# Router with high and low weights side by side, spare rows stored by slot, and loads moved at both ends of an attention and mixture-of-experts kernel

## What is computed

```python
xn = _layernorm(x)
# attention: 16 heads of 32, causal
P = softmax(where(causal, Q @ K.T * scale, -1e30)); out = (P @ V) @ Wo.T
# router: 8 experts in 4 groups of 2, the best 2 groups, then the best 2 experts
logits = xn @ rw.T
scores = sigmoid(logits)
sfc = scores + bias
...
topk_w = topk_w / (sum(topk_w) + 1e-20) * 2.5
# each expert, and a shared one of double width (704)
y_e = (silu(xn @ gate_e.T) * (xn @ up_e.T)) @ down_e.T        # 352 wide
```

## Time and profile before

| | |
|---|---|
| median of 3 runs | 1050.87 us |
| the three runs | 1046.09, 1050.87, 1958.02 us |
| the profiled execution | 1046.42 us |
| its span | 1044.7 us |
| busy: PE, DVE, ACT, POOL | 981.6, 725.4, 678.2, 533.8 us |
| granted PE clock, mean | 0.982 |

### The profile page before, as it was taken

One profiled execution on the slowest core, in us unless ns is written; L12 is line 12 of the kernel. 1 busy time (PEld: TensorE's weight loads), 2 busy tenths in 40 slices (PEclk: granted clock), 3 DMA queues, 4 the chain that ended last, 5 costly groups with the idle time before them and its releaser, 6 DMA issues. The chain is left out here.

```text
span 1044.7 us, 18885 instructions
## 1 busy us (share of the span) xinstructions
PE 981.6 (94%) x5176; PEld 808.7 (77%) x5177; DVE 725.4 (69%) x1436; ACT 678.2 (65%) x1419; POOL 533.8 (51%) x573
## 2 busy tenths in 40 slices
PE   5999988999999999999999999988879999999994
PEld 4767877787787877777777877766679999999993
DVE  6741332667687788888898888753467777777771
ACT  3332211278788897888888878871167777777771
POOL 0010840768788877876666766751013444434421
PEclk9999989999999999999999999999899999999997
DMA  6989897644787867969868778538889545465432
GB/s 202 331 320 383 228 205 266 204 134 96 192 159 172 174 138 177 202 143 268 247 199 247 206 247 199 171 117 290 294 283 310 100 91 123 93 173 89 77 59 38
DMA packets 136491, 199.69 MB, mean 191 GB/s; under 512 B 63088, under 2 KB 81776, under 8 KB 132816
## 3 DMA queue, kind: packets, MB, share of 16 engines
q1 hardware_dynamic: 126064, 177.88, 59.8%
q0 software_dynamic: 9760, 20.49, 10.6%
q10 hardware_dynamic: 576, 0.26, 0.2%
HBM read 117.11 MB, written 73.08 MB: 182 GB/s over the span
## 5 line engine op out<-in xcount | busy, mean ns | idle before, releaser
L1448 POOL TENSOR_TENSOR prob_lo<-prob,prob_hi 128x512 fp32r<-128x512 f32 (+2 forms) x320 | 329.7, 1048 | 127.1 <-ACT prob_hi L1492 114.8
L1485 ACT ACTIVATE prob<-ps_s 128x512 f32<-128x512 f32 (+3 forms) x384 | 188.1, 490 | 70.9 <-PE ps_s L1729 50.0
L1492 ACT ACTIVATE prob_hi<-prob 128x512 fp32r<-128x512 f32 (+3 forms) x384 | 199.4, 520 | 12.4 <-ACT row_stage L1466 12.4
L1581 DVE CUSTOM_DVE_ANT_0 ps_m<-ps_m,causal 128x384 f32<-128x384 f32 (+3 forms) x256 | 125.4, 497 | 55.3 <-PE ps_m L1700 48.5
L2140 DVE TENSOR_TENSOR rw_lo<-gu_sb,rw_hi 128x704 fp32r<-128x704 f32 x156 | 135.8, 892 | 34.7 <-ACT rw_hi L2072 32.6
L2072 ACT ACTIVATE rw_hi<-gu_sb 128x704 fp32r x156 | 123.5, 794 | 32.0 <-issue 21.8
L2045 POOL DMA_INDIRECT out<-work,slot_table x39 | 64.5, 1654 | 155.3 <-ACT work L2102 94.1
L1724 PE MATMUL ps_s<-qs,ks 97*128 97x512 f32 (+3 forms) x384 | 136.3, 355 | 3.2 <-DMA qs<-max_rows 2.2
L1700 PE MATMUL ps_m<-ks,qs 96*128 96x512 f32 (+3 forms) x384 | 131.3, 342 | 5.6 <-DVE maxima L1581 5.5
L1747 PE MATMUL ps_o<-prob_hi,vs 128*66 128x512 f32 (+3 forms) x384 | 130.0, 339 | 1.3 <-POOL prob_lo L1448 1.3
L1749 PE MATMUL ps_o<-prob_lo,vs 128*66 128x512 f32 (+3 forms) x384 | 129.3, 337 | 0.0
(11 more groups left out here) (207 smaller groups left out, 2358.3 us busy)
## 6 DMA issues: line engine op xcount, KB each, us to landing
xt<-xt_blocks SPq DMA_DIRECT2D x7, 2048.0 KB, 8.5
v_rows<-work SPq DMA_DIRECT2D x16, 512.0 KB, 3.1
xt_blocks<-xt SPq DMA_DIRECT2D x4, 2048.0 KB, 11.3
qk_hi<-work SPq DMA_DIRECT2D x8, 1024.0 KB, 4.5
qk_lo<-work SPq DMA_DIRECT2D x8, 1024.0 KB, 7.3
qs<-qk_hi SPq DMA_DIRECT2D x64, 128.0 KB
ks<-qk_hi SPq DMA_DIRECT2D x64, 128.0 KB
vs<-v_rows SPq DMA_DIRECT2D x32, 256.0 KB
```

Source lines behind the costliest of these rows:

```text
L1448: nc.gpsimd.tensor_tensor(prob_lo[:, s % NPL, 0:w], prob[:, s % NP, 0:w], prob_hi[:, s % NPH, 0:w].bitcast(F32), ALU.subtract).then_inc(lo ...
L1485: nc.scalar.activation(prob[:, s % NP, 0:w], bank("score", s)[:, 0:w], ACT.Exp, scale=SCALE).then_inc(exp_done, 1)
L1492: nc.scalar.activation(prob_hi[:, s % NPH, 0:w], prob[:, s % NP, 0:w], ACT.Copy).then_inc(hi_ready, 1)
L1581: nc.vector.tensor_tensor_reduce(ps_m[s % NM][:, 0:w], ps_m[s % NM][:, 0:w], causal[:, TBW - w:], 1.0, MASKED, ALU.add, ALU.max, maxima[:, ...
```

## The change

1. In norm_phase wv is loaded before tile 2 of x instead of before tile 1.
2. `r_hi` and `r_lo` become the two halves of `r_parts`, 16 columns. Each block takes 8 matmuls of 16 stationary columns. The copies, the transposes and the PSUM tile `ps_s` are 16 wide. VectorE copies one half of the turned logits and adds the other to it, at the head of its evacuation of chunk 1, and ScalarE's sigmoid waits for that.
3. The spare rows are made in a tile of their own, [39, 128, 2], one partition for each tile of slots, and stored as 39 rows of 1 KB at the same step.
4. The tiles of `out` for the first two steps of out_phase are loaded into `y_first` at the end of attend_phase, behind wo. out_phase doesn't load them again.
5. The first experts' loads are cut: gate, up, first down part, second down part at steps 4, 5, 6, 7 for expert 0 and 8, 9, 10, 11 for expert 1.

```diff
-FIRST_AT = [5, 9]
+FIRST_AT = [(4, 5, 6, 7), (8, 9, 10, 11)]
...
-        r_hi = ctx.enter_context(nc.sbuf_tensor("r_hi", [P, KC, E], F32R))
-        r_lo = ctx.enter_context(nc.sbuf_tensor("r_lo", [P, KC, E], F32R))
+        r_parts = ctx.enter_context(nc.sbuf_tensor("r_parts", [P, KC, 2 * E], F32R))
...
+            y_first = nc.alloc_sbuf_tensor_at("y_first", [P, 2, D], F32,
+                                              offset=nc.sbuf_base + 4 * TBW * KC)
...
+def load_matrix(eng, e, n, matrix, gu_sb, expert_loaded):
+    eng.dma_start(gu_sb[:, e * KC:(e + 1) * KC, n * F:(n + 1) * F],
+                  matrix[e * KC:(e + 1) * KC].rearrange("k p f -> p k f")
+                  ).then_inc(expert_loaded[e % len(FIRST_AT)], 16)
...
+def load_down_part(eng, e, part, down_dram, d_ring, down_loaded):
+    n, w, at = e % DOWN_SLOTS, FCH[-1][1], part * len(FCH)
+    eng.dma_start(d_ring[:, n, at:at + 2, :].bitcast(F32), down_dram[e, :, part, 0:2, :]
+                  ).then_inc(down_loaded[n], 16)
+    eng.dma_start(d_ring[0:w, n, at + 2, :].bitcast(F32), down_dram[e, 0:w, part, 2, :]
+                  ).then_inc(down_loaded[n], 16)
...
-                    if t == 1:
+                    if t == 2:
+
                         for k in range(KC):
                             sp.dma_start(wv_raw[:, k, :], wv[:, k, :]).then_inc(wv_loaded[k], 16)
...
-                        sp.dma_start(slots_dram.rearrange("(j p) a -> p j a", p=P),
-                                     slot_table[:, :, :]).then_inc(pads_stored, 16)
+                        sp.dma_start(slots_dram.rearrange("(j p) a -> j p a", p=P),
+                                     pads[:, :, :]).then_inc(pads_stored, 16)
...
                         if t == 1 and n == 1:
-                            act.wait_ge(logits_turned, 1)
-                            nc.scalar.activation(score[:, :, :], ps_s[:, :, :],
+                            act.wait_ge(logits_summed, 2)
+                            nc.scalar.activation(score[:, :, :], score[:, :, :],
                                                  ACT.Sigmoid).then_inc(score_ready, 1)
...
-                        for a, part in ((r_hi, 0), (r_lo, 0), (r_hi, 1)):
-                            last = nc.tensor.matmul(ps_r[0:E, :], a[:, k, :], xt[n][:, part, k, :],
-                                                    start=(j == 0), stop=(j == 3 * KC - 1))
+                        for part in range(2):
+                            last = nc.tensor.matmul(ps_r[0:2 * E, :], r_parts[:, k, :],
+                                                    xt[n][:, part, k, :],
+                                                    start=(j == 0), stop=(j == 2 * KC - 1))
...
-                nc.gpsimd.iota(pads[:, :], pattern=[[0, 1]], base=T, channel_multiplier=1
+                nc.gpsimd.iota(spare_rows[:, :], pattern=[[1, P]], base=T, channel_multiplier=0
                                ).then_inc(table_padded, 1)
-                nc.gpsimd.memset(slot_table[:, :, 1], 0.0).then_inc(table_padded, 1)
+                nc.gpsimd.memset(pads[:, :, 1], 0.0).then_inc(table_padded, 1)
                 pool.wait_ge(table_padded, 2)
-                nc.gpsimd.tensor_copy(slot_table[:, :, 0].bitcast(I32),
-                                      pads[:, :].broadcast_to([P, NST])).then_inc(table_padded, 1)
+                nc.gpsimd.tensor_copy(pads[:, :, 0].bitcast(I32), spare_rows[:, :]
+                                      ).then_inc(table_padded, 1)
...
                         dve.wait_ge(logits_turned, 1)
+                        nc.vector.tensor_copy(score[:, :, :], ps_s[:, :, E:]
+                                              ).then_inc(logits_summed, 1)
+                        dve.wait_ge(logits_summed, 1)
+                        nc.vector.tensor_tensor(score[:, :, :], ps_s[:, :, 0:E], score[:, :, :],
+                                                ALU.add).then_inc(logits_summed, 1)
...
+                def load_first_tokens():
+
+                    sp.wait_ge(acc_stored, 64 * (UNITS - NTB + 1))
+                    for t in range(OUT_AHEAD):
+                        sp.dma_start(y_first[:, t, :], out[t * P:(t + 1) * P, :]
+                                     ).then_inc(x_loaded[t], 16)
...
+                    if t < R:
+                        return
                     wait(sp, added, t - U + 1)
                     sp.dma_start(y_tile[:, c, :], out[bass.ds(t * P, P), :]).then_inc(x_loaded[c], 16)
...
-                    if isinstance(t, int) and t in FIRST_AT:
-                        e = FIRST_AT.index(t)
-                        load_expert(sp, e, gate, up, gu_sb, expert_loaded)
-                        load_down(sp, e, down_dram, d_ring, down_loaded)
+                    for e, at in enumerate(FIRST_AT):
+                        for n, matrix in enumerate((gate, up)):
+                            if t == at[n]:
+                                load_matrix(sp, e, n, matrix, gu_sb, expert_loaded)
+                        for part in range(2):
+                            if t == at[2 + part]:
+                                load_down_part(sp, e, part, down_dram, d_ring, down_loaded)
...
+                    tokens = y_first if t < R else y_tile
+                    nc.vector.tensor_tensor(y_sum[:, c, :], ps_y[c % R][:, :], tokens[:, c, :],
                                             ALU.add).then_inc(added, 1)
```

More of the change, by code:

```diff
@@ L187, in moe_attention_kernel @@
                 norm_phase(nc, x, wv, wqk, xt, w_raw, w_loaded, ident, v_dram, xn_dram, out, work,
-                           v_stored, xn_stored, zeros_stored, router, r_hi, r_lo, passed, x_loaded)
+                           v_stored, xn_stored, zeros_stored, router, r_parts, passed, x_loaded)
                 second_half = Half(*[finish_ctx.enter_context(
@@ L219, in moe_attention_kernel @@
                 nc.sbuf_tensor("y_tile", [P, YS, D], F32) as y_tile:
-            out_phase(nc, finish, wo_hi, wo_lo, out_hi, out_lo, a_hi_ready, a_lo_ready, gate, up, down_dram, ident, work, gu_sb, d_ring, out, y_tile, y_stored,
+            out_phase(nc, finish, wo_hi, wo_lo, out_hi, out_lo, a_hi_ready, a_lo_ready, gate, up, down_dram, ident, work, gu_sb, d_ring, out, y_tile, y_first, y_stored,
                       slot_table, xn_dram, gathered, passed, expert_loaded, w_loaded, x_loaded)
@@ L323, in row_numbers @@
     return bass.IndirectOffsetOnAxis(slot_table[:, j, 0:1].bitcast(I32), 0)
+def load_matrix(eng, e, n, matrix, gu_sb, expert_loaded):
+    eng.dma_start(gu_sb[:, e * KC:(e + 1) * KC, n * F:(n + 1) * F],
+                  matrix[e * KC:(e + 1) * KC].rearrange("k p f -> p k f")
+                  ).then_inc(expert_loaded[e % len(FIRST_AT)], 16)
 def load_expert(eng, e, gate, up, gu_sb, expert_loaded):
[L327 to L330, removed]
+    for n, matrix in enumerate((gate, up)):
+        load_matrix(eng, e, n, matrix, gu_sb, expert_loaded)
 def downs_loaded(e):
@@ L338, in downs_loaded @@
     return W_BEFORE + raw + 64 * (e // DOWN_SLOTS + 1)
+def load_down_part(eng, e, part, down_dram, d_ring, down_loaded):
[4 more added lines that the diff above has]
+                  ).then_inc(down_loaded[n], 16)
 def load_down(eng, e, down_dram, d_ring, down_loaded):
-    n, w = e % DOWN_SLOTS, FCH[-1][1]
     for part in range(2):
[L345 to L349, removed]
+        load_down_part(eng, e, part, down_dram, d_ring, down_loaded)
 def norm_phase(nc, x, wv, wqk, xt, w_raw, w_loaded, ident, v_dram, xn_dram, out, work, v_stored,
-               xn_stored, zeros_stored, router, r_hi, r_lo, passed, x_loaded):
+               xn_stored, zeros_stored, router, r_parts, passed, x_loaded):
     with ExitStack() as ctx:
@@ L590, in project_phase @@
         bias_b = sbuf("bias_b", [P, 1, E])
-        pads = sbuf("pads", [P, 1], I32)
+        spare_rows = sbuf("spare_rows", [NST, P], I32)
+        pads = sbuf("pads", [NST, P, 2])
         score = sbuf("score", [P, NT, E])
@@ L604, in project_phase @@
         ps_r = psum("ps_r", [P, TBW])
-        ps_s = psum("ps_s", [P, NT, E])
+        ps_s = psum("ps_s", [P, NT, 2 * E])
         ps_rank = psum("ps_rank", [P, NT, E])
```

25 lines of the change are left out of this document (14 added, 11 removed).

## The result

The changed kernel took 1036.28 us in the median of six runs (1034.43 to 1040.53). The kernel before took 1051.48 beside them, also in the median of six: five from 1045.71 to 1053.69 and one of 1958.02. The ratio is 0.985, its 95% interval 0.982 to 0.988. The forecast was 1030.5 with a range of 1022 to 1040, and "within 2%" at 0.79. The time lies in the range and in the likeliest class, 5.8 us above the forecast and 1.3 above the forecast's own range. In this series the measured gain, 15.2 us, is close to the sum of the forecast, 15.9, and what was off is the time from which the sum was subtracted.

A forecast was written before the change was run, and what follows sets the result against it. It took TensorE (PE) as the bound, at 94% of its span, and subtracted 1.2 + 3.7 + 6.0 + 5.0 = 15.9 us from 1046.4 to get 1030.5. Its own range was 1027 to 1035, widened by rivals to 1022 to 1040.

The forecast's parts named there:

- A: Kernel start: loading wv after the second x tile brings the first value matmul from 14.11 to 12.9; gain 1.2 us.
- B: Projection: the 16-column router needs 16 fewer matmuls at 0.232 us each; gain 3.7 us, from 2.3 to 3.7.
- C: Projection: storing spare rows by slot removes a stall of 3.42 us standing and 2.6 at lower clock; gain 6.0 us.
- D and E: Output stage: two out tiles loaded early (D, 0 to 0.3 us) and first experts' loads cut (E); gain 5 us.
- no y_tile wait over 2 us: Output stage: sign expected for the early tiles and cut loads, no wait for a y_tile load above 2 us.
- 9 us are to be had: Output stage: PE's loss to expert loads, 5.24 + 1.40 us standing and 2.3 at the lower clock level.
- some 4.5 us of the 9 stay: Output stage: loss expected to remain because DMA at 334 GB/s needs 3.7 us per step where PE wants 2.80.
- (2): Output stage: short waits lower PE's clock over three or four tiles, taking the stage's gain; about 1036 us, chance 0.10.
- (3): Output stage: clock stays at the lower level from tile 5 to 15, slower than before; 1051.7 us, chance 0.02.
- Rival (1): Output stage: DMA engines carry some 400 GB/s, no wait is left, 9 us gained; 1026.5 us, chance 0.14.
- The base: Whole kernel: the time subtracted from, the profiled execution's 1046.4 us, instead of the median shown, 1050.87.
- Attention and the routed stage keep their lengths within 2 us: Attention and routed experts: sign that these stages change by at most 2 us; the prediction is wrong if they move.

The follow-up runs named there:

- e4: The changed kernel with twelve 8-column router matmuls per block again and no sum of halves; 1040.65 us.
- e2: The kernel before with only the spare rows stored by slot; 1049.14 us, ratio 0.9925.
- e5: The kernel before, unedited, run once more for a second profile; 1055.45 us (one run).
- e9: The kernel before, unedited, timed against itself in twelve runs; 1055.13 us, ratio 0.998.
- e3: The kernel before with only the first experts' loads cut into steps 4 to 11, without the early load of out tiles; 1049.3 us, ratio 0.997.
- e1: The changed kernel, unedited, run again for a second profile; 1036.68 us, ratio 0.980 to the kernel before.
- e8: The changed kernel, unedited, run a third time; 1036.11 us, ratio 0.981 to the kernel before.
- e7: The changed kernel with attention's 2 MB loads of turned tokens cut into four of 512 KB, three steps apart; 1036.1 us.
- e6: The changed kernel with expert 1's four load pieces at steps 12 to 15 instead of 8 to 11; 1035.15 us, ratio 0.979 to the kernel before.
- e10: The changed kernel with the experts' load pieces at steps 2, 4, 6, 8 and 10, 12, 14, 15; 1034.2 us, ratio 0.978 to the kernel before.

## Why the prediction was right

**What bounds the kernel.** Right within what the profiles tell: the time of PE standing or slow that the edits removed came off its stages, 6.15 us for a forecast 6.0 in projection and 4.3 in the output stage, where PE's losses fell by 4.5.

**A.** "Gain 1.2." The first pair gave 0.9 at the first value matmul (14.11 to 13.20). Over all profiles the five with the old start had it at 13.66 to 14.17 (mean 13.98), the nine with the new one at 11.61 to 13.20 (mean 12.15): 1.8 us, and as much at the first router matmul. Right in kind and inside its ends, 0.6 too small. The term is tile 2's landing: I put it at 10.2, and VectorE took the tile up at 9.05 to 10.64, 9.60 in the mean.

**B.** "3.7." Right: 3.7 in e4's profile, and 4.0 in the medians, which spread more than that. The pitch stayed, and VectorE's two operations (0.29 each) delayed neither PE nor ScalarE: none of their listed waits in the stage is for them.

**C.** "Gain 6.0; ends 3 and 6.3." Right: 6.15 in the projection of e2; 6.9 us (1056.01 to 1049.14) in the medians. The upper end was read from one draw of the stall: PE stood 3.42 us for it in the first profile and 4.53, 4.42 and 5.43 in the other three with the old store (e5, e9, e3). The stores of chunks 3 and 4, which I saw as next late, held nobody. The landing of the new store, put at 3 to 5 us, isn't recorded; that no wait on `ps_q` is left and 288 GB/s move from 124 to 140 is what shows it harmless. One sign failed, "a granted clock of 1.00 there": it was 0.83 in the stage's first 10 us, though not by the store. It costs about 1.5 us, and that is why the pair of profiles shows 8.3 us where B and C measured 3.7 + 6.15.

**D and E.** "Gain 5; ends 1 and 9." Measured 4.3 in the first pair, 4.6 and 4.5 with e1 and e8 against the same profile; e4 and e7, with the same output stage, would give 2.3 and 4.0. What D gives (forecast 0 to 0.3) is lost in that spread. The sign "no y_tile wait over 2 us" failed by one wait of VectorE, 2.59 us, with PE never held as long. Seven more waits at VectorE's add, 14.8 us in sum, are listed without what ended them; that the pieces hold the steps is shown by e6 and e10, which only moved them. The terms can be read from PE's pitches. One held step of the kernel after, PE in the timeline:

```profile
725.02 0.40 PE L1975 MATMUL ps_ay<-wo_lo,a_hi 128*128 128x512 f32 x1
725.25 0.40 PE L1975 MATMUL ps_ay<-wo_hi,a_lo 128*128 128x512 f32 x1
726.04 0.50 PE L1975 MATMUL ps_ay<-wo_hi,a_hi 128*128 128x512 f32 x1 [0.39 <-DVE a_lo L1936]
726.38 0.39 PE L1975 MATMUL ps_ay<-wo_lo,a_hi 128*128 128x512 f32 x1
```

Pitches are 0.233 us when nothing holds PE. Here they are 0.79 and then 0.34: 0.56 + 0.11 = 0.67 us lost, where the bracket reads 0.39. Each restart costs some 0.27 us beyond its idle time: 0.40 - 0.233 = 0.17, since a matmul lasts longer than the pitch, and 0.11 for the slower first pitch. Summed in this way over the steps that were held, seven of them (two too short to be listed), the kernel after loses 4.9 us. In before the two stalls lose 7.1 by the same reading and the slow stretch behind the first 2.3 more (11 pitches in 4.86 us, 733.28 to 738.14, where 2.56 would do): 9.4. So "9 us are to be had" was 9.4, "some 4.5 us of the 9 stay" was 4.9, and 9.4 - 4.9 = 4.5 against 4.3 measured. The second figure is right by two errors that cancel. The engines carried more than the 334 GB/s that I took: 385, 345, 379, 374 and 353 in the five windows that had loads to the end, 367 in the mean, so PE idled less, 2.8 us listed. And I counted nothing for restarts, seven times 0.27 or 1.9 us.

That short waits leave the clock alone held in this stage: after five waits of up to 0.8 us, seven in e3 and seven of up to 1.07 in e4, it read 1.00. Rivals (2) and (3) fell with that. The frequent short idle times between groups that the Trainium skill (TensorE: Matmul & The Clock Gate, A second HAM failure mode: psum-queue depth-cycling) describes as making the clock swing did not do so here. It isn't a matter of length alone: 1.13 us in attention was followed by 0.50 in e9 and by 1.00 in the profile before. Rival (1) was half right on the rate and wrong on "no wait is left"; e10 reached that by giving the pieces room.

**The base: the step that was off.** "The lowest, 1046.09, agrees with the profiled one, so I forecast from there." Two executions that agree and happen to be the fast ones are no base for a median. 1051.48 - 15.9 = 1035.6 and would have met 1036.28. The median of 1050.87 stood in the table and the 4.5 us between it and my base are most of the miss of 5.8. That the time still fell into the range is luck in part. In the later series the kernel before has 1055.8 to 1056.0, and the gain was 19.3 and 19.7 us (e1, e8): against them my base was 9.3 to 9.6 too low and my sum 3.4 to 3.8 too small, and the two errors work against each other. Where the surplus lies stays open. A's 0.6 us and the longer stalls of C are candidates, but the spans of the three profiles of each kernel differ by no more than 13.9 us in the mean (1050.6 and 1036.8), so the surplus stands in the medians alone. A lucky draw can be seen in the profile before, once others are there to compare: PE's waits for `max_rows` are 2.2 us against 5.0 and 5.4 in e5 and e9, and its clock stays full behind the idle times of 2.74 and 1.13 us early in attention. The first alone doesn't tell: e1 has 2.8 us of such waits and 531.4 us of attention.

**"Attention and the routed stage keep their lengths within 2 us."** Failed for attention in the pair of profiles (+6.4; the routed stage's +1.0 is within it). For the kernels no shift is shown: 524.0, 531.0 and 532.9 (mean 529.3) against 530.4, 531.4 and 528.3 (mean 530.0). Taken as a test of the change, the sentence asked one execution for what only several can show.

## What to carry to other kernels

Subtract a forecast from the median of the runs, and check by stage whether the profiled execution is a typical one: where a stage has many idle times of a microsecond or two, on late transfers or on other engines, profiles of one kernel can differ by 9 us in it, as attention did here. More than half of that can be PE working at the lower clock behind an idle time that left it alone in another execution. A comparison of two profiles needs a second profile of each before a stage that nobody edited is explained. Loads that a later stage needs are best spread so that each step's bytes fit into its compute time with a pause between them: 16 tiles of 2.8 us hid eight loads almost wholly at every other step, and at consecutive ones only half of the time lost before was won back. And a wait of PE costs more than its length: a restart took 0.27 us more here at full clock, and 2.3 to 2.6 us more where the clock fell.

## What the runs showed of the hardware

- A store of 4992 elements of 8 bytes, 39 KB, took 22.2 us to land; while it ran, two windows of 4 us carried 7 and 24 GB/s with the DMA engines full (128 to 136). With the same bytes in rows of 1 KB these windows carried 328 and 131 GB/s and nothing waited.
- In the output stage the 16 DMA engines carried up to 404 GB/s in 5 us (e10, 720 to 725), with loads and stores mixed.
- One idle time, two outcomes for TensorE's clock. PE stood 2.15 us ahead of projection in all fourteen profiles; the granted clock in the stage's first 10 us was 0.83 in six (after, e1, e4, e5, e8, e10) and 1.00 in the other eight. Behind the 2.7 us ahead of attention it fell in eleven (not in before, after and e7), behind the 1.13 us at head 1 in three. In projection it costs about 1.5 us (101.3 to 101.4 against 99.8 in the changed kernel and its variants). What decides it stays open.
- In attention single loads came late at changing places: PE stood up to 4.01 us for a 4 KB row (after), ScalarE 2.30 us for `gu_raw` (e1) and 5.49 us for `d_raw` (e7). Most heads took 14.4 to 16.4 us from the second on; these three took 22.3, 20.8 and 20.1.
